# Set-up of the second attention: part of it in the linear stage, half of it inside the first unit of scores

## The reference

```
Q = (x @ W_k.T).reshape(B, S, 16, 8).transpose(0, 2, 1, 3)
sq_norm = sum(Q * Q, axis=-1)
scores = -(sq_norm - 2 * Q Q^T + sq_norm^T) / sqrt(8)
context_q = softmax(scores) @ Q
merged = einsum('hkd,hvd->hkv', W_k per head, W_v per head)
attn_out = context_q @ merged / sqrt(8)
return attn_out @ W_o.T
```

## Time and profile before

| what | us |
|---|---|
| median of 3 runs | 1182.9 (1182.59 to 1183.47) |
| the profiled execution, its own time | 1174.82 |
| its span | 1173.0 |
| TensorE busy | 1071.4 (91%) |
| VectorE busy | 770.1 (66%) |
| ScalarE busy | 719.8 (61%) |
| GpSimd busy | 541.1 (46%) |

### The profile page before, as it was taken

One profiled execution on the slowest core, in us unless ns is written; L12 is line 12 of the kernel. 1 busy time (PEld: TensorE's weight loads), 2 busy tenths in 40 slices (PEclk: granted clock), 3 DMA queues, 4 the chain that ended last, 5 costly groups with the idle time before them and its releaser, 6 DMA issues.

```text
span 1173.0 us, 16993 instructions
## 1 busy us (share of the span) xinstructions
PE 1071.4 (91%) x5839; PEld 584.6 (50%) x5839; DVE 770.1 (66%) x1547; ACT 719.8 (61%) x1173; POOL 541.1 (46%) x446
## 2 busy tenths in 40 slices
PE   4699999999999999999956799999999579999998
PEld 2445555455455545555536422222322258778876
DVE  5767877777787777777545322225221379999998
ACT  4345555555565565555422499998999466666663
POOL 1356666666656666666630000000000126788786
PEclk9789999999999999999976699999999879999999
DMA  4111111111111111110200000000000002112110
GB/s 123 27 26 37 43 33 37 43 32 31 44 43 26 44 43 26 37 44 20 64 0 1 3 8 12 12 12 9 10 11 10 10 0 93 58 69 76 67 54 37
DMA packets 35290, 40.30 MB, mean 34 GB/s; under 512 B 19652, under 2 KB 22484, under 8 KB 34188
## 3 DMA queue, kind: packets, MB, share of 16 engines
q1 hardware_dynamic: 35212, 39.30, 13.0%
HBM read 19.23 MB, written 1.11 MB: 17 GB/s over the span
## 4 chain that ended last, share of the span: by engine, by line
PE 59%; DVE 27%; issue 9%; SPq 1%; ACT 1%; POOL 1%; DMA 1%; DVEq 0%; ACTq 0%; POOLq 0%
PE banks L1003 10%; PE banks L400 8%; PE banks L991 6%; PE banks L345 5%; PE banks L385 5%; DVE qb L1308 5%; PE banks L321 5%; PE banks L386 4%; PE banks L421 3%; PE banks L366 3%; DVE kb L581 2%; DVE banks L601 2%; DVE qa L581 2%; DVE zz L630 2%; DVE qb L610 2%
## 5 line engine op out<-in xcount | busy, mean ns | idle before, releaser
L710 POOL TENSOR_TENSOR pacc<-pacc,prob 128x1024 f32<-128x1024 f32 (+3 forms) x160 | 274.0, 1712 | 64.4 <-ACT prob L512 55.1
L1012 ACT ACTIVATE prob<-banks 128x1024 f32<-128x1024 f32 x256 | 238.7, 1094 | 22.1 <-PE banks L991 22.1
L512 ACT ACTIVATE prob<-banks 128x512 f32<-128x512 f32 (+3 forms) x384 | 167.8, 488 | 113.4 <-PE banks L386 111.8
L1341 POOL TENSOR_TENSOR ka<-prob,qb 128x512 fp32r<-128x512 f32 x108 | 165.0, 1549 | 59.6 <-ACT qb L1291 33.1
L385 PE MATMUL banks<-qa,ka 128*128 128x512 f32 (+3 forms) x384 | 150.7, 400 | 1.3 <-ACT prob L512 1.3
L400 PE MATMUL banks<-prob,v 128*64 128x512 f32 (+3 forms) x768 | 145.0, 498 | 1.0 <-POOL prob L701 1.0
L1297 ACT ACTIVATE prob<-banks,w 128x512 f32<-128x512 f32 x144 | 94.7, 687 | 71.3 <-PE banks L1259 71.3
L1003 PE MATMUL banks<-prob,v 128*32 128x512 f32 x1024 | 137.1, 608 | 0.8 <-DVE pacc L1020 0.3
L386 PE MATMUL banks<-qb,kb 72*128 72x512 f32 (+3 forms) x384 | 131.5, 350 | 0.0
L957 POOL TENSOR_TENSOR sq<-sq 64x512 f32<-64x512 f32 x8 | 8.3, 1033 | 261.3 <-DVE sq L953 261.3
L701 POOL TENSOR_SCALAR_AFFINE_SELECT prob<-prob 128x256 f32<-128x256 f32 x128 | 52.1, 407 | 147.6 <-ACT prob L512 145.9
(11 more groups left out here) (211 smaller groups left out, 1610.7 us busy)
## 6 DMA issues: line engine op xcount, KB each, us to landing
qb<-qa SPq DMA_DIRECT2D x64, 128.0 KB, 2.3
ka<-ka SPq DMA_DIRECT2D x64, 128.0 KB, 2.3
prob<-gate_rows SPq DMA_DIRECT2D x8, 1024.0 KB, 4.7
w<-in_experts SPq DMA_DIRECT2D x9, 514.0 KB, 3.5
wqkv<-in_wqkv SPq DMA_DIRECT2D x16, 193.0 KB, 2.4
x<-in_x SPq DMA_DIRECT2D x4, 256.0 KB, 4.1
zz<-pacc SPq DMA_DIRECT2D x64, 16.0 KB
wpr<-pacc SPq DMA_DIRECT2D x64, 16.0 KB
```

The costliest lines, as they stand in the source:

```text
L512: act.activation(pr[:, j % NRING, h, 0:wd], banks[:, h, 0:wd], ACT.Exp, scale=SCALE0).then_inc(s_exp, 1)
L710: pool.tensor_tensor(pacc[:, sbk, :, o:BLK], pacc[:, sbk, :, o:BLK], pr[:, j % NRING, :, 0:wd], ALU.add).then_inc(s_padd, 1)
L1012: act.activation(prob[:, n % NP1, :], banks[:, 2 * (n % 3):2 * (n % 3) + 2, :].rearrange("p b c -> p (b c)"), ACT.Exp, scale=2 * SCALE1).t ...
L1341: pool.tensor_tensor(act2[1][:, tb % 2, i, :], hid[:, tb % 2, i, :], act2[0][:, tb % 2, i, :], ALU.subtract).then_inc(s_hlP, 1)
```

## The change

The masked product of the weights (L891, L916, L901, L910) goes to the linear stage: the first product ahead of the down-projections, the second behind them and ahead of the base products, VectorE's memset of qv and its mask ahead of the router chain, ScalarE's store behind the two stores of dn.

In the set-up, heads and qtm of the first batch start when two groups of xT are there, not four. TensorE makes qtm groups 0 and 1 (one batch's worth), then projection and norm of half 0 alone, then qtm groups 2 and 3. VectorE fills the sides of half 0, the values, then half 1. The first scores wait for half 0 alone (s_rl 4); call j = 8 waits for half 1 (s_rl 8). Projection and norm of half 1 stand in the first unit behind its first two score calls, and the first unit's heads, projection 0 and norm 0 for the next unit stand two steps later (i = 4, 6, 7). The qtm groups use banks 4, 5, 2, 3.

```diff
         def linear_pe(pe):
+            pe.wait_ge(s_aw, 48)
+            pe.matmul(banks[:, 6, 0:P], wvT[:, :], wkT[:, :], start=True, stop=True).then_inc(s_a1, 1)
             for n in range(NT):
                 if n % 4 == 0:
                     pe.wait_ge(ln[1]["xT"], n // 4 + 1)
...
+            pe.wait_ge(s_a1m, 1)
+            pe.matmul(banks[:, 7, 0:D], a1[:, :], woT[:, :], start=True, stop=True).then_inc(s_gg, 1)
             for n in range(NT):
                 pe.matmul(banks[:, n // 4, (n % 4) * P:(n % 4 + 1) * P], xT[:, n * P:(n + 1) * P], wbase[:, :], start=(n % 4 == 0), stop=False)
+            pe.wait_ge(s_gge, 1)
             pe.wait_ge(s_ch, N_CHAIN)
...
                 act.activation(dn[:, i * TB:(i + 1) * TB, :].rearrange("p n c -> p (n c)"), banks[:, 4 + i, 0:TB * DALL], ACT.Copy)\
                    .then_inc(s_dne, 1)
+            act.wait_ge(s_gg, 1)
+            act.activation(gg[:, :], banks[:, 7, 0:D], ACT.Copy).then_inc(s_gge, 1)
             act.wait_ge(s_ch, 4)
...
+            dve.memset(qv[:, :, :, :, :].rearrange("p b t h j -> p (b t h j)"), 1.0).then_inc(s_qv, 1)
+            dve.wait_ge(s_a1, 1)
+            dve.scalar_tensor_tensor(out=a1[:, :], in0=banks[:, 6, 0:P], scalar=SCALE1, in1=cst[:, C_BD:C_BD + P],
+                                     op0=ALU.mult, op1=ALU.mult).then_inc(s_a1m, 1)
             dve.wait_ge(s_dne, 2)
...
+        QT_BANK = (4, 5, 2, 3)
+
+        def qtm_pe(pe, i):
+            for t in range(4):
+                n = 4 * i + t
+                mm = pe.matmul(banks[:, QT_BANK[i], t * P:(t + 1) * P], xT[:, n * P:(n + 1) * P], wkT[:, :], start=True, stop=True)
+            mm.then_inc(s_qt, 1)
+
         def setup1_pe(pe):
-            pe.wait_ge(s_aw, 48)
+            pe.wait_ge(ln[2]["xT"], 2)
+            heads1_pe(pe, 0)
+            for i in range(2):
+                qtm_pe(pe, i)
+            proj1_pe(pe, 0, 0, 7)
+            norm1_pe(pe, 0, 0, 7)
             pe.wait_ge(ln[2]["xT"], 4)
-            heads1_pe(pe, 0)
...
+            for i in range(2, 4):
+                qtm_pe(pe, i)
...
         def setup1_dve(dve):
...
             prep1_dve(dve, 0)
...
+            sides1_dve(dve, 0, 0, 7)
             dve.wait_ge(s_qv, 1)
-            dve.wait_ge(s_qte, 4)
+            dve.wait_ge(s_qte, 2)
             values1_dve(dve, 0)
-            for hf in range(2):
-                sides1_dve(dve, 0, hf, 7 - hf)
+            sides1_dve(dve, 0, 1, 7)
...
-            if j == 0:
+            if u == 0 and j in (0, TB):
+                pe.wait_ge(s_rl, 4 if j == 0 else 8)
+            elif u == 0 and j == 1:
+                pe.wait_ge(s_qte, 4)
+            elif j == 0:
                 pe.wait_ge(s_rl, 8 * (u + 1))
...
+                    if u == 0 and i == 0:
+                        proj1_pe(pe, 0, 1, 7)
+                        norm1_pe(pe, 0, 1, 7)
                     if u < NB1 - 1:
-                        if i == HEADS_AT:
+                        late = 2 if u == 0 and i < TB else 0
+                        if i - late == HEADS_AT:
                             heads1_pe(pe, u + 1)
```

## The result

The changed kernel takes 1167.19 us, the median of 17 runs (1164.12 to 1177.3). The kernel before, run beside it, takes 1175.75, also of 17 (1173.3 to 1183.92). The ratio is 0.9927, 95% interval 0.9907 to 0.9947. So the change makes it 8.6 us faster, where 8.5 was forecast; but the time itself was forecast as 1174.4, with a range down to 1172.2 only. The gain was right and the base was not: the three runs shown ahead (1182.59 to 1183.47) were all long ones of the kernel before. They are among its 17 runs, of which only 5 lie above 1182. The profiled execution after took 1166.66, its span 1164.8, against 1164.5 by the forecast (1173.0 - 8.5).

What follows compares the result with a forecast made beforehand. TensorE was taken to bound the second attention, so starting it sooner at full clock helps. 6.25 + 3.8 - 0.2 - 1.3 = 8.5 us gain; 1182.9 - 8.5 = 1174.4 us, range 1172.2 to 1178.2.

Steps and rivals of the forecast that it cites:

- the last of the sum: Whole kernel: the 8.5 us gain subtracted from the runs' median of 1182.9, giving 1174.4.
- What bounds it: Second attention: TensorE, busy 31.38 of 31.45 us in a full unit, sets the pace; ScalarE is busy 29.86.
- Linear stage, +0.5 for the product ahead: First product ahead of the down-projections adds 0.5 us (bounds 0.45 and 0.73); the other moved parts are covered.
- Set-up, 6.75 to the first score: Set-up: first score at about 659.0 in place of 665.77, 6.75 us earlier, or 6.25 less the linear stage's 0.5.
- 1.11 for two against 0.69 for one: Norms in the set-up: two take 1.11 us, one 0.69, so splitting them gives up a pairing.
- Start of the attention, 3.8 back and 1.3 moved in: First unit: 3.8 us regained if the clock holds, 0.2 lost waiting for exponentials, 1.3 for half 1's projection and norm.
- Slack: First unit: 1.6 us spare before call j = 8, 3 for the head weights, 0.6 before projection 1.
- the four: Late clock (0.20); clock low into first unit (0.05); half not worth it (0.03); slower, half 1's sides late (0.04).

Runs made afterwards that it cites:

- the product alone: The kernel before with only the linear stage's part of the diff, the masked product of the weights moved there: 1175.26 us, ratio 0.9996.
- The filler: The kernel before with 24 needless 128x128 matmuls in TensorE's rest behind the norms, while VectorE makes the sides: 1171.18 us, ratio 0.9979.

## Why the prediction was right in its gain and wrong in its time

**The step that failed** is the last of the sum: "The median of the runs is 8.1 above it, a difference that the profile doesn't explain and that I carry over". The gain of 8.5 us was subtracted from 1182.9, the median of three executions that were all long, and the range was built around that alone. Subtracted from the profiled execution's own 1174.82 it gives 1166.3, and 1167.19 was measured. Nothing in the range stood for the base itself being off, although a profile 8 us below all three runs said that this kernel has at least two durations. What separates them in the kernel before isn't settled: in three profiles of its variants it was the clock, low at several places ahead of layer norm 1, with one fall late in the causal attention worth 3.2 us; no execution of the kernel before itself above 1178 has a profile.

**The gain is partly luck.** Its parts were off in both directions. By the two profiles the linear stage gave 0.6 where 0.5 was to be lost, the set-up gave 7.9 where 6.75 was forecast, the start of the attention 1.7 where 2.3 was, and the fifth unit took back 2.1 that the forecast doesn't have. The sum is 8.2 against 8.5, though each of these parts is off by 0.6 to 2.1. At the second unit's heads the changed kernel was 10.2 ahead, not 8.5; that the whole comes out beside the forecast is those parts cancelling, in these two executions.

**What bounds it**: right. A full unit takes 31.45 us before and after, with the clock at 1.00.

**Linear stage, +0.5 for the product ahead**: right in size; the product alone cost 0.5, and 0.43 on the chain after. VectorE's and ScalarE's parts were hidden, as forecast. That the profile after has this stage 0.6 shorter is the clock's: down-projections 4.16 for 6.71, turns at L808 3.39 for 1.92.

**Set-up, 6.75 to the first score**: the mechanism was right (one half of the sides ahead of it, no pause, no product between), the size 1.2 too small. The clock rose at about 650.2 after, ahead of most of qtm 0 and 1, so that they took 2.12 us in place of 3.6. One norm by itself was 1.07 on the chain, not 0.69. The 0.69 was a misreading: the earlier trace rows shows one of the norm's two records, and the second is this one of the kernel before:

```profile
680.14 0.59 PE L949 MATMUL banks<-sq,cst 32*128 32x512 f32 x1
```

From the start of the first to the end of the second it is 1.12 us. So "1.11 for two against 0.69 for one" should read 1.11 for two, each with two records, against 1.07 for one: the pairing that the prediction gives up is worth more than it says.

**Start of the attention, 3.8 back and 1.3 moved in**: this is the mis-sized term. The filler shows 2.6 with the clock up, where 3.8 - 0.2 = 3.6 was forecast. The stepping through the calls had TensorE wait 0.2 for exponentials, and it waits 0.88 + 0.42 + 0.42 = 1.72 before calls 3, 4 and 5: nothing else stands in its list there. No clock can bring that back. Projection and norm of half 1, put at 1.3, cost about 0.6, since most of them lies in those waits, and 0.29 of waiting for VectorE is new. The sum is 2.6 - 0.6 - 0.3 = 1.7 instead of 2.3. The Trainium skill (TensorE: Matmul & The Clock Gate, Part 3: Packing small matmuls) lets a norm hide behind a score call of other rows. The trace agrees so far as that both were recorded starting together, at 658.77 and 658.78; no run here separates what this brings from what ScalarE's pace hides.

**Slack**: call j = 8 never waited, the head weights were there in time, with no wait on a DMA before L940. At projection 1 of the next unit 0.6 us of slack was forecast, and TensorE waits 0.29: the norm ends 1.13 after it starts, not 0.69, and VectorE still needs its 3.07 behind it.

**Not foreseen**: the +2.1 us in the fifth unit, a wait of the old order whose size hangs on SP's issue times and behind which the clock can fall. It fell behind waits of 1.54 and 1.70 us, and not behind one of 1.65 in the kernel before.

**Rivals**: none of the four came true. The clock was not late, and the sides of half 1 stopped nothing.

## What to carry to other kernels

When the profile shown takes noticeably less or more than the runs shown, forecast the difference, and let the range for the time hold both durations; one median of three runs is one draw of a kernel that has several. A serial preparation in front of a bounded stage is best cut by the half that its first instructions need; the other half can go into the stage's first steps, where the follow-on engine sets the pace for a while, and where it cost about 0.6 us here for 1.9 us of work. A rest of TensorE costs its own length and then the slow clock behind it, 2.6 us here for a rest of 5.75; a wait for results that came through a DMA queue should stand a step later than it can just be met.

## What the runs showed of the hardware

The clock rose at different moments of the same work. The down-projections took 6.71, 6.71 and 4.16 us in three executions with the same instructions ahead of them, or nearly the same, and turns of another group 1.92 or 3.39. The same wait of 1.59 us in the causal attention had the clock fall in 3 of 16 profiles, at 3.2 us each. So in single profiles a stage that has not been touched can differ by 1 to 3 us.

Three DMA issues of the same small tile took SP 1.47 to 2.83 us. Where a chain of DMAs stands behind them, that difference arrives in full: in the 14 profiles with the first output projection at step 0, TensorE's wait there (0.33 to 1.70 us) is the time from the first to the end of the fourth issue less 1.7.

The kernel's executions spread over 10 us. In five profiles, two of them long, the start-up ran products at twice the usual duration while the granted clock of the view still read 1.00; there the durations of the instructions themselves told more than the clock's column.
